# One decoder on one core: two joined seams, root placement, a distance table moved to POOL's idle tail, and a lighter POOL in the gated layer

## The reference, cut to what matters

```python
# layer 5: which experts, then one projection per batch of rows
pooled = hidden_states.mean(axis=1)
logits = relu(pooled @ Wg1 + bg1) @ Wg2 + bg2
weights = softmax over the top 2 of logits          # 0 elsewhere
Wc = einsum('be,ecd->bcd', weights, W); bc = weights @ b
q, k, v = (hidden_states @ Wc + bc for W, b in (q, k, v))
# layer 6: the local scores get a distance times a slope per head
scores = scores + dist[None, None] * slopes[None, :, None, None]
# layer 9
xr = gelu(lin) * scan(a, sqrt(1 - a * a) * (it * x)) @ W_lin2.T + b_lin2
residual = xr + residual
y = (gelu(sigmoid(xm @ W1.T + b1)) * (xm @ W2.T + b2)) @ W3.T + b3
return y + residual
```

## Time and profile before

| | |
|---|---|
| median of 3 runs | 3982.16 us (3981.55 to 3984.32) |
| the profiled execution's own time | 3982.85 us |
| its span | 3981.0 us |
| mean granted TensorE clock | 0.958 of full |
| busy share | PE 91%, DVE 77%, ACT 57%, POOL 36% |
| the chain that ended last | PE 55%, DVE 19%, ACT 5%, issue 4%, POOL 1% |
| seam of layers 0 and 1 | 1018 to 1057 us |
| layer 4 | 2425 to 2575 us |
| seam of layers 4 and 5 | 2557 to 2601 us |
| seam of layers 5 and 6 | 2831 to 2873 us |
| layer 9 | 3467 to 3620 us |

### The profile page before, as it was taken

One profiled execution on the slowest core, in us unless ns is written; L12 is line 12 of the kernel. 1 busy time (PEld: TensorE's weight loads), 2 busy tenths in 40 slices (PEclk: granted clock), 3 DMA queues, 4 the chain that ended last, 5 costly groups with the idle time before them and its releaser, 6 DMA issues.

```text
span 3981.0 us, 57266 instructions
## 1 busy us (share of the span) xinstructions
PE 3627.7 (91%) x19890; PEld 2550.7 (64%) x19890; DVE 3072.0 (77%) x7103; ACT 2253.5 (57%) x5322; POOL 1427.7 (36%) x928
## 2 busy tenths in 40 slices
PE   6888988999899989999999999788798889989998
PEld 2334334344566768997888897555566568746877
DVE  7999989999787667667888787778577785565777
ACT  7576776776665532223555555578678662254446
POOL 4989888999200000000333234477321200030000
PEclk8998999999999999999999999889999999999999
DMA  4555545657521000000000001000000000100000
GB/s 146 160 152 161 174 150 174 189 182 233 195 86 48 29 25 22 33 12 16 1 1 1 1 1 45 16 1 1 13 2 1 21 25 1 47 0 23 1 1 22
DMA packets 145015, 240.33 MB, mean 60 GB/s; under 512 B 23400, under 2 KB 67696, under 8 KB 142040
## 3 DMA queue, kind: packets, MB, share of 16 engines
q1 hardware_dynamic: 114051, 212.75, 17.2%
q10 hardware_dynamic: 30676, 23.93, 1.8%
HBM read 210.08 MB, written 26.54 MB: 59 GB/s over the span
## 4 chain that ended last, share of the span: by engine, by line
PE 55%; DVE 19%; ACT 5%; issue 4%; POOL 1%; ACTq 0%; DVEq 0%; POOLq 0%
PE PS L209 44%; PE PS L216 8%; DVE db L1315 3%; PE PS L1984 3%; DVE stat L291 1%; DVE p L4004 1%; ACT PS L1280 1%; DVE qg L2481 1%; PE PS L3616 1%; DVE db L1320 1%; DVE p L2495 1%; DVE XNr L328 1%; DVE W L2758 0%; DVE p L3058 0%; POOL far L4146 0%
## 5 line engine op out<-in xcount | busy, mean ns | idle before, releaser
L1315 DVE TENSOR_TENSOR_SCAN db<-PS,db 128x512 f32<-128x512 f32 x512 | 591.7, 1205 | 46.3 <-ACT PS L1280 33.4
L209 PE MATMUL PS<-db,cst 128*128 128x512 f32 x1024 | 500.6, 629 | 26.0 <-DVE db L1320 26.0
L216 PE MATMUL PS<-cst,p 128*128 128x128 f32 (+1 forms) x2880 | 397.9, 284 | 53.5 <-DVE pt L3580 14.7
L2288 POOL TENSOR_TENSOR rb<-rb,tb 128x512 f32<-128x512 f32 x32 | 43.0, 1342 | 1088.7 <-DVE tb L2283 1088.7
L216 PEld LDWEIGHTS PS<-cst,p 128*128 128x128 f32 (+1 forms) x2880 | 332.6, 147 | 128.0 <-issue 61.1
L209 PEld LDWEIGHTS PS<-db,cst 128*128 128x128 f32 x1024 | 202.8, 202 | 289.1 <-issue 237.2
L209 PE MATMUL PS<-xnT,W 128*128 128x256 f32 (+2 forms) x880 | 324.3, 511 | 37.5 <-ACT gate L1112 15.3
L1261 POOL TENSOR_TENSOR db<-W,b 128x1024 f32<-128x1024 f32 x128 | 307.3, 2427 | 59.7 <-DVE W L1197 45.3
L1261 POOL TENSOR_TENSOR db<-du,b 128x1024 f32<-128x1024 f32 x128 | 305.9, 2416 | 37.7 <-PE PS L209 37.0
L209 PEld LDWEIGHTS PS<-xnT,W 128*128 128x128 f32 (+1 forms) x880 | 168.9, 197 | 165.3 <-issue 113.8
L2139 ACT ACTIVATE W<-PS,W 128x512 f32<-128x512 f32 x144 | 98.7, 689 | 288.7 <-PE PS L209 270.9
(11 more groups left out here) (479 smaller groups left out, 8428.4 us busy)
## 6 DMA issues: line engine op xcount, KB each, us to landing
b<-bc_rows SPq DMA_DIRECT2D x256, 256.0 KB, 3.8
c<-bc_rows SPq DMA_DIRECT2D x256, 256.0 KB, 4.0
qk<-fore_qk SPq DMA_DIRECT2D x48, 294.5 KB, 2.9
fore_qk<-W ACTq DMA_DIRECT2D x48, 256.0 KB, 4.3
W<-in_we SPq DMA_DIRECT2D x9, 1024.0 KB, 4.9
W<-in_w SPq DMA_DIRECT2D x50, 128.0 KB, 3.7
fore_v<-W ACTq DMA_DIRECT2D x24, 256.0 KB, 3.2
v<-fore_v SPq DMA_DIRECT2D x6, 1024.0 KB
```

Of the source, the lines that this page charges most:

```text
L209: ins = T.matmul(out, l, r, start=first and i == 0, stop=last and i == len(pairs) - 1)
L216: ins = T.transpose(bank[0:m, c:c + r], s, ident[0:r, 0:r])
L1315: V.tensor_tensor_scan(db[:, f, r], self.ring.PS[:, self.BANKS[x % 3], r], db[:, f, r], 0.0, ALU.mult, ALU.add).then_inc(self.sc.sem, 1)
L2288: e.eng.tensor_tensor(self.rb[t % 2], self.rb[t % 2], self.tb[t % len(self.tb)], ALU.add).then_inc(self.rg.sem, 1)
```

## The change

It has five parts.

**Seam of layers 0 and 1.** The scores of units 0 and 1 are issued by PE between the last sums of layer 0, with maxima, exponentials and normalisation of those units in layer 0's last steps; `back_each` gives each PSUM bank back under a token of its own; the loop of layer 1 begins at step 2 (`begin`). The sums of the last state units are made one unit earlier (`sums`). The heads of all eight units of the first batch and its values are loaded ahead. The norm of chunk 3, which started at step -1, starts at step 3.

**Roots in layer 4.** For chunks 0 to 2 `act_roots` issues the square root in the next step, behind the first half of its exponentials.

**Seam of layers 4 and 5.** `GATE` issues four of the gate's pieces one step earlier; QK of batch 0 is issued ahead of the output of batch 7; the scores of unit 0 and the masked keys are made in layer 4's tail; `MIXV` comes behind the maxima of unit 0; POOL makes zero, the bias and the keys first and the two memsets of v afterwards.

**far.** `pool_fars` makes the table at the end of layer 5's POOL stream, in four tiles of its own.

**Layer 9.** The product buf4 * buf2 is DVE's (phase `MUL`, last of its step), R to X is one 128 x 1024 addition per chunk on DVE (`dve_keep`), and the eight row additions are issued by POOL in two bursts, three and five, at phase 8 of chunks 0 and 1 (`POOL_ROWS`).

```diff
+    def back_each(self, freed):
+        assert sorted(j for j, _ in freed) == sorted(j for j, _ in self.kept)
+        for j, token in freed:
+            self.freed[j] = (token,)
+            self.free.append(j)
...
-            if 1 <= d <= k:
+            if 1 <= d <= k and c not in self.amid:
                 self.act_sd(e, c, d - 1)
...
+    def act_roots(self, e, step, ends):
+        for c, s in ends.items():
+            if c in self.amid and step == s + 2:
+                self.act_sd(e, c, 0)
...
-        self.nxt.late, self.nxt.dense = {3: -1}, True
+        self.nxt.late, self.nxt.dense = {3: 3}, True
...
     def sums(self, t):
+        if t >= self.NU - 1:
+            return [t - 2, t - 1] if t < self.NU else [t - 1]
...
+            if i - 2 == self.NU - 1:
+                self.ring.back_each(self.last_reads())
+                self.after.pe_scores(e, 0, (0,))
+            elif i - 2 == self.NU:
+                self.after.pe_scores(e, 0, (1,))
             if 0 <= i - 2 <= self.NU:
                 self.pe_tail(e, i - 2)
+        self.after.pe_scores(e, 1)
         for t in range(12, 16):
             self.pe_out(e, t)
             self.ring.release(("x", 0, t), self.x(t + 1))
-        self.ring.back(self.made(self.NU - 1))
...
+        for u in range(self.after.BEFORE):
+            self.after.act_exp(e, u)
...
+        self.after.dve_max(e, 1)
+        self.after.dve_norm(e, 0)
         for j in range(4):
             self.dve_to_x(e, 12 + j)
+            if j == 1:
+                self.after.dve_norm(e, 1)
...
-            self.ahead = 4096 // (S + self.NK)
+            self.ahead = F
...
     def sp_ahead(self, e):
+        M = self.prev
+        for u in range(self.ahead):
+            if u == self.BEFORE:
+                e.wait_ge(*M.aa(2 * M.NU))
+                e.wait_ge(*M.gb(M.NU))
+            for token in self.fore.head_stored(u):
+                e.wait_ge(*token)
+            self.sp_heads(e, u)
         for token in self.fore.stored():
             e.wait_ge(*token)
-        for u in range(self.ahead):
-            self.sp_heads(e, u)
+        e.wait_ge(*M.ys(M.NU))
+        self.sp_values(e, 0)
...
+    GATE = {"pe": {15: (1,), 16: (2,)}, "act": {15: (1,), 16: (3,)}, "dve": {14: (0,), 15: (2,), 16: (3,), 17: (4,), 18: (5,)}}
...
-        self.nxt.late = {3: -1}
+        self.nxt.late, self.nxt.amid = {3: -1}, (0, 1, 2)
...
             if r == 1 and 0 <= b < NB:
+                if self.follow and b == NB - 1:
+                    self.follow.pe_open(e)
                 self.pe_end(e, b)
             if self.follow:
-                self.follow.pe_gate(e, 0, s - 14)
+                for k in self.GATE["pe"].get(s, ()):
+                    self.follow.pe_gate(e, 0, k)
+        if self.follow:
+            self.follow.pe_scores_open(e)
...
             if g in (1, 2) and u >= 2:
                 self.act_copy(e, u - 2, 2 * g - 2)
+            if g == 1:
+                self.nxt.act_roots(e, u, self.nxt.early)
...
                 self.dve_max(e, s + 1)
+            if self.opened(s + 1):
+                for x in range(4):
+                    self.dve_piece(e, 0, self.MIXV, x)
...
+    def pool_open(self, e):
+        e.wait_ge(*self.prev.mx(4 * self.prev.NU))
+        e.wait_ge(*self.prev.s(4 * self.prev.NU))
+        e.eng.memset(self.zero, 0.0).then_inc(self.zz.sem, 1)
+        self.pool_bias(e, 0)
+        self.pool_keys(e, 0)
...
+    def pool_fars(self, e):
+        M = self.prev
+        e.wait_ge(*self.w_ready)
+        e.wait_ge(*M.s(4 * M.NU))
+        e.wait_ge(*M.mx(4 * M.NU))
+        e.wait_ge(*M.pv(NB))
+        for r in range(4):
+            self.pool_far(e, r)
...
-    DVE_ORDER = (5, 15, 3, 13, 6, 7, 9, 11, 0, 2, 12, 17, 18)
+    DVE_ORDER = (5, 15, 3, 13, 6, 7, 9, 11, 0, 2, 12, 17, 18, MUL)
+    POOL_ROWS = {0: ((0, "r"), (0, "x"), (1, "x")), 1: ((1, "r"), (2, "x"), (3, "x"), (2, "r"), (3, "r"))}
+    KEEP = (15, 16, 15, 16)
...
-                if p == 9:
-                    e.wait_ge(*self.iA(2 * c + 2))
-                    e.wait_ge(*self.xcD(2 * c + 2))
-                    G.tensor_tensor(buf[4], buf[4], buf[2], ALU.mult).then_inc(self.qG.sem, 1)
...
-                elif p == 12:
-                    e.wait_ge(*self.qG(2 * c + 1))
-                    for j in range(4):
-                        t = 4 * c + j
-                        e.wait_ge(*self.r2(t + 1))
-                        e.wait_ge(*self.x_in(t))
-                        G.tensor_tensor(X[:, t, :], X[:, t, :], R[:, j, :], ALU.add).then_inc(self.xg.sem, 1)
+                if p == 8 and c in self.POOL_ROWS:
                     e.wait_ge(*self.rowS(2))
+                    e.wait_ge(*(self.pm["conv"](3) if c else self.pm["a"](1)))
+                    for c2, kind in self.POOL_ROWS[c]:
+                        self.pool_row(e, c2, kind)
...
+    def dve_keep(self, e, c):
+        X = self.E.X[:, 4 * c:4 * c + 4, :]
+        e.wait_ge(*self.rowX(c + 1))
+        e.wait_ge(*self.r2(4 * c + 4))
+        for t in range(4 * c, 4 * c + 4):
+            e.wait_ge(*self.x_in(t))
+        e.eng.tensor_tensor(X, X, self.R[c], ALU.add).then_inc(self.xg.sem, 1)
...
+            V.tensor_tensor(buf[4], buf[4], buf[2], ALU.mult).then_inc(self.ixD.sem, 1)
```

175 lines of the change are left out of this document (117 added, 58 removed).

## The result

The changed kernel takes 3958.58 us in the median of 4 runs (3954.88 to 3964.35), against 3983.24 for the kernel before in the same comparison (3981.55 to 3987.28). The ratio is 0.9937, with a 95% interval of 0.9923 to 0.9951. That is 24.7 us less, where 36 were forecast; the time lies inside the range. None of the nine came nearer to 3946 than 3954.88. The profiled execution has a span of 3954.7 us, 26.3 less than before, at a mean granted clock of 0.964.

A forecast was written before the change was run, and what follows sets the result against it. The prediction took TensorE (PE) as the bound, at 55% of the chain of waits, with DVE at 19%. Terms 10.8 + 8 + 5 + 4.8 + 7.4 = 36.0 us gave 3946 us in the median, range 3934 to 3966.

The forecast's parts named there:

- The longer switch of tables: Seam of layers 0 and 1: a drain of about 1.38 us per table switch would cut the term to 5 us.
- then delays the values: Seam of layers 4 and 5: moved v mixing (last part 2.77 us) delays values; 5 of 7.9 us taken as gain.
- QK of layer 5 without a wait of 5 us: Sign in the profile that the forecast is right: layer 5's QK starts without its former wait of 5.44 us.
- The 1.5 for the rope products: Seam of layers 5 and 6: first rope products come later by up to 3 us, of which 1.5 counted.
- The 0.7 for the copy rr: Layer 5's last batches: 0.7 us given back because POOL's instructions now run beside the copy rr.
- the 5.65 us: Layer 9: four cnT applications fall from 6.85 to 1.2 us, shortening the stretch behind PE's 6.74 us wait.
- The 1.2 that the DVE additions were to give back: Layer 9: one DVE addition, of chunk 1, stands ahead of the next layer's statistics and costs 1.2 us.
- third rival: POOL's bunched row additions hold DVE up to 10 us in layer 9, far's sixteen layer 5; 3955 us, chance 0.12.
- The rule that I weighed against this step: DVE in two-port mode or with two SBUF inputs and GpSimd take one port pair in turn, per whole instruction.
- first rival: Pipelines take the gain back, each term at its lower end, ACT returning 11.3 us in layer 1; 3966, chance 0.12.
- fourth rival: Seam of layers 0 and 1 doesn't join, units 0 and 1 no earlier; without the 10.8, 3957 us, chance 0.07.
- clock rival: Layer 1: gaps in units 3 to 8 drop TensorE to 1.2 GHz and it stays; 15 units give 4012, chance 0.04.

The follow-up runs named there:

- again: The changed kernel run once more, unchanged, for a second profile; 3964.46 us, ratio 0.9947.
- mixv_early: The changed kernel with the v weights mixed ahead of the q conversions again, in DVE's idle 3.62 us; 3958.40 us, ratio 0.9929.
- mixv_row: mixv_early with POOL's first row addition to X moved behind the mixing and keys of batch 1; 3957.15 us, ratio 0.9933.
- best: mixv_row and the spread row additions of g_spread together; 3954.34 us, ratio 0.9925.
- g_spread: The changed kernel with POOL's eight row additions in layer 9 spread over four places (three, two, two, one); 3958.32 us, ratio 0.9938.
- u_seam01: The changed kernel with the seam of layers 0 and 1 as before the change, all else kept; 3976.65 us, ratio 0.9973.

## Why the prediction was right, and where its size was off

The direction and the five places were right, and so was the way the parts win time; what each part gives back was priced too low in three of them. The sum was 11 us too large against the median of the first series and 16 against all nine executions. Step by step:

- **Seam of layers 0 and 1**, forecast 10.8, found 11.0 or 11.1 in five profiles, again's among them, and 8.2 or 8.3 in six. Where the sums kept the full pace (again) the first values came 15.6 earlier (15.2 in the sum) and 4.6 was handed back (4.4 in the sum), so the term was right to a few tenths. In the first profile it was 14.1 and 5.8. The sum had nothing for half pace behind the 2.00 us wait for POOL's product and behind the roots, which cost what the earlier trace rows said. The longer switch of tables that the Trainium skill gives (ScalarE: Activation LUTs, what ACT_TABLE_LOAD costs) isn't borne out: the load at 2488.95 starts 0.02 us behind the copy ahead of it, and the root at 2490.25 follows the load's 1.28 us at once.
- **Roots**, forecast 8, found 7.1; 6.4 by taking the part out. The first root gave 5.8 for 5, the second 1.9 for 3.
- **Seam of layers 4 and 5**, forecast 5, found 3.3 (2.1 to 3.8 in others) and 1.4 to 3.1 by taking it out. What was mis-sized is "then delays the values", which I named and gave no price of its own: 3.60 us of wait, shown by mixv_early, which removed it. The sign "QK of layer 5 without a wait of 5 us" did not come either: 6.37 us, since QK now stands ahead of the last output matmuls. What stood behind the wait for the v weights, POOL's row addition waiting for a DMA, I had not seen; mixv_row and best show it (steps of 5.2 and 7.3).
- **far**, forecast 4.8, found 5.5, and 3.7 to 5.7 in the table's other kernels (0.4 of it without the part). The 1.5 for the rope products was exact (2.94 less 1.48). The 0.7 for the copy rr was not paid: it kept 0.43 us beside POOL.
- **Layer 9**, forecast 7.4, found 3.7 or 3.8 in three profiles and 0.4 to 0.9 in six. TensorE's two idle stretches, 3.13 and 7.82 before, became shorter by 8.0 us together, as forecast; but the stretch that the 5.65 us shorten is the 7.82, not the 6.74 that the prediction names. The 1.2 that the DVE additions were to give back were 3.0. The third rival came true at its place, for 4.1 us instead of 10: the burst held DVE by the lock. I had judged that TensorE had matmuls queued there; it waited 2.84 us. g_spread shows that the burst was the cause, and with it gone the layer gives 7.7 and 7.8 (g_spread, best). The rule that I weighed against this step (the Trainium skill, SBUF — State Buffer, two separate sides) agrees with these rows; it should have gone into the term and not only into a rival.
- **Unforecast**: layer 0 ended 3.2 us later in the changed kernel's profile with the same code, and between 0.3 earlier and 2.3 later in the seven others of the table (1.2 earlier in mixv_row). The code of layer 0 is the same in all up to its last sums, so this is spread between executions. It hides a tenth of the gain in one comparison.

The first rival's time (all terms at their lower ends, 3966) was nearer to both series of this kernel, 3958.6 and 3964.5, than the forecast, though the terms were not all at their lower ends and ACT did not give its 11.3 us back. That the times of the third and fourth rival, 3955 and 3957, lie nearer still to the first series is chance: the burst cost 4.1 us of the third's 10, and the seam joined. The clock rival did not happen as written: single gaps cost 1.6 to 3 us, and the layer always came back.

What stays open: why TensorE's pace falls behind a given gap in one execution and not in the next (the rows show that it does, not what decides it), and where the median of u_seam01 lost 10 us on its profiled execution.

## What to carry to other kernels

When an engine that shares a lock with DVE is relieved, look at where its remaining work is bunched: four instructions of 128 x 4 and 128 x 1024 grew by 1.6, 1.8, 0.6 and 1.7 us because five POOL additions ran in one piece, and spreading them over DVE's waits took it back. Work moved off one wait should land in another engine's idle stretch; the v mixing left one of 3.62 us and made one of 3.60. And for changes of some tenths of a per cent, compare the start of the same instruction in two profiles: the steps of that offset that the code makes repeat to half a microsecond (the burst 4.0 and 4.1, most roots 6.6 to 7.1) where medians swing by six. Compare all kernels at the same instruction, and expect steps with a wait in them to take one of two values, as the seam of layers 0 and 1 did with 8.3 and 11.0.

## What the runs showed of the hardware that was not expected

The same kernel differed by 10 us between executions (3954.9 to 3964.8). The profiles of all the kernels place such differences: up to 4.4 us in layer 0 (mixv_row and the changed kernel), and 1.5 to 4 us at single places at which a group of matmuls ran at half its pace behind an idle stretch, or didn't, in otherwise equal rows (5.09 and 6.77 us for the same 16). Short waits are enough: behind 2.0 us for POOL the same eight sums took 3.70 us in five profiles and 5.40 in seven. And the lock is selective: beside POOL a DVE product of 128 x 4 elements took 1.92 us instead of 0.16, while two instructions that read PSUM behind it (1.40 for both) and, in other places, four bn_stats (1.41, kernel before) and the copy rr (0.43) kept their times.
